# The self neighbour's part of a window graph convolution: per pair from gathered values, or per chunk from y with one matrix

## The reference

```python
feat = concat([x_i, x_j - x_i])          # x_i the node, x_j each of its 9 neighbours
h = einsum('bnkc,oc->bnko', feat, ew) + eb
h = gelu(h * es + et)                    # O = 192 channels
h = max(h, axis=2)                       # over the 9 neighbours
x = affine(conv1x1(window_reverse(h), fc2)) + x
```

## Time and profile before

| | |
|---|---|
| median of 3 runs | 4308.5 us (4302.23 to 4312.94) |
| profiled execution | 4302.27 us, its span 4300.5 us |
| TensorE clock, mean granted | 0.992 |
| busy: PE / DVE / ACT / POOL | 4078.2 / 4077.2 / 3620.3 / 538.3 us (95 / 95 / 84 / 13%) |
| L586 and L592 (self matmuls) | 284.6 and 144.9 us in records of 261 and 219 ns |
| L769 (self GELU) | 262.3 us |
| L941 (maxima) | 992.9 us, 1939 ns each |

### The profile page before, as it was taken

How to read it: one execution, slowest core, us unless ns; L and a number is a source line. 1 busy time by engine, 2 the same in 40 slices (tenths; PEclk the granted TensorE clock), 3 DMA queues, 4 the chain that set the end, 5 groups by cost and what they waited for, 6 DMA issues and landing times.

```text
span 4300.5 us, 84159 instructions
## 1 busy us (share of the span) xinstructions
PE 4078.2 (95%) x26688; PEld 2423.2 (56%) x26688; DVE 4077.2 (95%) x5296; ACT 3620.3 (84%) x7141; POOL 538.3 (13%) x548
## 2 busy tenths in 40 slices
PE   5999999999999999999999999999999999999994
PEld 2555555555555555555555555555555555555552
DVE  2599999999999999999999999999999999999998
ACT  3888888888888888888888888888889888888873
POOL 0011111011111011111011111111111111110100
PEclk9999999999999999999999999999999999999997
DMA  1111121111111111120111111111111111211111
GB/s 48 23 31 33 25 45 18 33 38 30 35 31 31 27 38 32 26 44 16 36 36 24 43 27 32 29 33 34 29 40 20 37 33 25 45 18 25 31 21 24
DMA packets 52989, 134.11 MB, mean 31 GB/s; under 512 B 7778, under 2 KB 9058, under 8 KB 46372
## 3 DMA queue, kind: packets, MB, share of 16 engines
q0 software_dynamic: 28672, 50.35, 8.2%
q1 hardware_dynamic: 23876, 78.22, 6.8%
HBM read 77.68 MB, written 25.69 MB: 24 GB/s over the span
## 4 chain that ended last, share of the span: by engine, by line
PE 61%; ACT 13%; issue 12%; DVE 12%; DMA 0%; SPq 0%; DVEq 0%; ACTq 0%; POOL 0%; POOLq 0%
PE pg L572 15%; DVE acc L954 9%; PE pmisc L498 8%; PE pmisc L482 8%; PE pg L575 7%; PE pvu L559 7%; ACT MV L746 3%; PE pself L586 3%; ACT acc L779 2%; PE pmisc L450 2%; ACT g L763 2%; PE pmisc L500 2%; PE pvu L545 2%; PE pmisc L443 2%; PE pmisc L465 1%
## 5 line engine op out<-in xcount | busy, mean ns | idle before, releaser
L954 DVE SCALAR_TENSOR_TENSOR acc<-hpad,w,acc 128x1024 f32<-128x1024 f32 (+1 forms) x2560 | 2911.9, 1168 | 89.1 <-ACT acc L779 86.0
L572 PE MATMUL pg<-MV,VU 128*128 128x512 f32 x2048 | 1143.8, 640 | 15.6 <-ACT VU L754 14.8
L763 ACT ACTIVATE g<-pg 128x512 f32<-128x512 f32 x1536 | 916.0, 596 | 144.3 <-PE pg L575 75.7
L941 DVE TENSOR_REDUCE hid<-g 128x192 f32<-128x1728 f32 x512 | 992.9, 1939 | 0.0
L746 ACT ACTIVATE MV<-pvu,cst 64x512 f32<-64x512 f32 x1024 | 695.6, 679 | 12.4 <-PE pvu L545 0.2
L482 PE MATMUL pmisc<-x,w 96*128 96x384 f32 (+1 forms) x1536 | 571.6, 487 | 23.1 <-ACT hpad L693 18.5
L575 PE MATMUL pg<-MV,VU 128*64 128x512 f32 x2048 | 527.5, 592 | 0.0
L498 PE MATMUL pmisc<-acc,w 128*96 128x256 f32 x2048 | 494.8, 385 | 30.2 <-ACT acc L786 30.2
L693 ACT ACTIVATE hpad<-pmisc,sh,sc 128x384 f32<-128x384 f32 (+1 forms) x768 | 480.6, 661 | 20.1 <-DVE acc L954 12.7
L559 PE MATMUL pvu<-wVU,y 97*64 97x192 f32 x4096 | 446.6, 339 | 30.6 <-ACT MV L746 30.1
L498 PEld LDWEIGHTS pmisc<-acc,w 128*96 128x96 f32 x2048 | 331.2, 164 | 212.4 <-issue 108.6
(11 more groups left out here) (95 smaller groups left out, 4231.9 us busy)
## 6 DMA issues: line engine op xcount, KB each, us to landing
xin<-in_x_dram SPq DMA_DIRECT2D x32, 768.0 KB, 5.7
invb<-rows_dram SPq DMA_DIRECT2D x32, 768.0 KB
x<-in_x_dram POOLq DMA_DIRECT2D x128, 192.0 KB, 3.6
res<-x POOLq DMA_DIRECT2D x128, 192.0 KB, 3.5
out_dram<-res SPq DMA_DIRECT2D x128, 192.0 KB, 2.1
g<-in_consts_dram SPq DMA_DIRECT2D x1, 640.0 KB
w<-in_p_dram SPq DMA_DIRECT2D x1, 618.5 KB
rows_dram<-norm_rows SPq DMA_DIRECT2D x32, 16.0 KB, 1.4
```

The lines of the kernel that those rows point to most:

```text
L572: last = nc.tensor.matmul(ps[:, :], VU[:, r, part, 0:ONE128], cols[part], start=True, stop=True)
L763: nc.scalar.activation(g[:, p % 2, part, :, 0:KN], pg[(3 * p + part) % 2][:, :].rearrange("p (n k) -> p n k", k=KN), ACT.Gelu).then_inc(ge ...
L941: nc.vector.tensor_reduce(hid[:, c % 2, j, :, :], g[:, r], op=ALU.max, axis=AX.X).then_inc(hid_ready, 1)
L954: nc.vector.scalar_tensor_tensor(out=dst, in0=src, scalar=wk, in1=dst, op0=ALU.mult, op1=ALU.add).then_inc(tap_done, 1)
```

## The change

The self neighbour's part of a node needs no gather: with x_j - x_i zero it is one matrix times y. A third matrix is added to wVU (es times the first half of ew, with the bias row), and two new kinds of shared job, one pair of jobs per chunk (4 pairs of windows): `self_full` multiplies the first 128 channels by all 512 nodes of the chunk, `self_half` the remaining 64 channels by the 256 nodes of each window side, into the two halves of the output partitions. ScalarE applies GELU while it empties the bank, into a new tile gself. They lie in slots 2 and 3 (even chunks) and 4 and 5 (odd chunks) modulo 8, ahead of fc2, w1 and w2 in ORDER.

MV and g lose their ninth place, `self_full`, `self_half` and `gelu_self` of each pair go, and `maxima` reduces over 8 and waits for the last gather's GELU. A new VectorE operation, `join_self`, takes the maximum of the four pairs' hid and gself (two tiles of 128 x 768) once per chunk, right behind the maxima of the chunk's last pair; fc2 waits for it. The transpose gets a bank of its own and loses the wait for the self GELU.

```diff
+SELF_AT = {2: 'self_half', 3: 'self_full', 4: 'self_half', 5: 'self_full'}
+ORDER = ('ssq', 'fc1', 'inv', 'self_full', 'self_half', 'fc2', 'w1', 'w2')
...
+    if p % SLOTS in SELF_AT and valid(b, B):
+        jobs.append((SELF_AT[p % SLOTS], b, p // PPC))
...
-        MV = sb("MV", [128, 2, 2, (KN + 1) * NODES])
-        g = sb("g", [128, 2, 3, NODES, KN + 1])
+        MV = sb("MV", [128, 2, 2, KN * NODES])
+        g = sb("g", [128, 2, 3, NODES, KN])
+        gself = sb("gself", [128, 2, PPC, 3, NODES])
...
+                elif kind == "self_full":
+                    bi, c = job[1:]
+                    last = nc.tensor.matmul(ps[:, :], wVU[:, 2, 0:ONE128], y[:, c, :], start=True, stop=True)
+                elif kind == "self_half":
+                    bi, c = job[1:]
+                    yc = y[:, c, :].rearrange("p (q win n) -> p q win n", q=PPC, win=2)
+                    for w in range(2):
+                        last = nc.tensor.matmul(ps[64 * w:64 * w + 64, 0:PPC * NODES].rearrange("p (q n) -> p q n", q=PPC),
+                                                wVU[:, 2, ONE128:O], yc[:, :, w, :], start=True, stop=True)
...
-                if due(count := P - 2):
-                    pe.wait_ge(self_gelu, count)
...
-            def self_full(P, p):
-                r = p % 2
-                if due(count := P):
-                    pe.wait_ge(self_gelu, count)
-
-                pe.wait_ge(featT_evac, P + 3 if not isinstance(P, int) else min(P + 3, NPAIRS))
-                for w in range(2):
-                    nc.tensor.matmul(pself[:, 64 * w:64 * w + 64], VU[:, r, w, 0:ONE128], MV[:, r, w, KN * NODES:],
-                                     start=True, stop=True)
-
-            def self_half(P, p):
-                r = p % 2
-                for w in range(2):
-                    last = nc.tensor.matmul(pself[64 * w:64 * w + 64, 128:192], VU[:, r, w, ONE128:O],
-                                            MV[:, r, w, KN * NODES:], start=True, stop=True)
-                last.then_inc(self_ready, 1)
...
+                elif kind == "self_full" or kind == "self_half":
+                    bi, c = job[1:]
+                    if kind == "self_half":
+                        if due(count := CHUNKS * bi + c - 1):
+                            act.wait_ge(chunk_ready, count)
...
+                    nc.scalar.activation(dst, src, ACT.Gelu).then_inc(misc_evac, 1)
...
-            def gelu_self(P, p):
-                act.wait_ge(self_ready, P + 1)
-                nc.scalar.activation(g[:, p % 2, :, :, KN],
-                                     pself[:, 0:192].rearrange("p (c n) -> p c n", c=3),
-                                     ACT.Gelu).then_inc(self_gelu, 1)
...
             def maxima(P, p):
                 c, j, r = (p % PAIRS) // PPC, p % PPC, p % 2
-                if due(count := P + 1):
-                    dve.wait_ge(self_gelu, count)
+                if due(count := 3 * P + 3):
+                    dve.wait_ge(gelu_done, count)
                 nc.vector.tensor_reduce(hid[:, c % 2, j, :, :], g[:, r], op=ALU.max, axis=AX.X).then_inc(hid_ready, 1)
+
+            def join_self(b, p, bc, c):
+
+                if due(count := PAIRS * bc + PPC * (c + 1)):
+                    dve.wait_ge(hid_ready, count)
+                fb, fp = when(b, p, 3 if c % 2 else 1)
+                dve.wait_ge(misc_evac, job_at(fb, fp, "self_full", c))
+                dve.sem_inc(dve_passed, 1)
+                nc.vector.tensor_tensor(hid[:, c % 2], hid[:, c % 2], gself[:, c % 2], ALU.max).then_inc(chunk_ready, 1)
...
+                    if p % PPC == 0:
+                        bc, c = (b, p // PPC - 1) if p else (b - 1, CHUNKS - 1)
+                        if valid(bc, B):
+                            join_self(b, p, bc, c)
```

More of the change, by code:

```diff
@@ L48 @@
 TAP_COUNTS = [5, 4, 5, 5, 5, 5, 6, 5]
-ORDER = ('ssq', 'fc1', 'inv', 'fc2', 'w1', 'w2')
+SELF_AT = {2: 'self_half', 3: 'self_full', 4: 'self_half', 5: 'self_full'}
+ORDER = ('ssq', 'fc1', 'inv', 'self_full', 'self_half', 'fc2', 'w1', 'w2')
 ADD_AT = {o + 1: q for o, q in W2_AT.items() if q % 2 == 1}
@@ L194, in build @@
         c16 = sb("c16", [128, C16], f16)
-        wVU = sb("wVU", [C + 1, 2, O])
+        wVU = sb("wVU", [C + 1, 3, O])
         l0sc = sb("l0sc", [C, 2])
@@ L255, in build @@
         pscore = pb("pscore", [128, 512])
-        pself = pb("pself", [128, 512])
+        pfeat = pb("pfeat", [128, 512])
         pvu = pb("pvu", [128, 512])
@@ L276, in build @@
             "featT_ready", "featT_evac", "onehot_in", "onehot_ready"))
-        vu_ready, vu_evac, gather_ready, self_ready, gelu_done, self_gelu = (sem(n) for n in (
-            "vu_ready", "vu_evac", "gather_ready", "self_ready", "gelu_done", "self_gelu"))
+        vu_ready, vu_evac, gather_ready, gelu_done, chunk_ready = (sem(n) for n in (
+            "vu_ready", "vu_evac", "gather_ready", "gelu_done", "chunk_ready"))
         sp_passed, pool_passed, dve_passed = sem("sp_passed"), sem("pool_passed"), sem("dve_passed")
@@ L459, in shared_job @@
                     bc, c = job[1:]
-                    if due(count := PAIRS * bc + PPC * (c + 1)):
-                        pe.wait_ge(hid_ready, count)
+                    if due(count := CHUNKS * bc + c + 1):
+                        pe.wait_ge(chunk_ready, count)
                     hc = hid[:, c % 2]
@@ L529, in feature_transpose @@
                     pe.wait_ge(feat_ready, count)
-                if due(count := P - 2):
-                    pe.wait_ge(self_gelu, count)
                 if due(count := P):
                     pe.wait_ge(featT_evac, count)
-                nc.tensor.matmul(pself[:, 256:320], feat[:, p % 2, :], I2,
+                nc.tensor.matmul(pfeat[:, 0:NODES], feat[:, p % 2, :], I2,
                                  start=True, stop=True).then_inc(featT_ready, 1)
@@ L569, in gather @@
                 r = p % 2
-                cols = [MV[:, r, w, 0:KN * NODES] for w in range(2)]
+                cols = [MV[:, r, w, :] for w in range(2)]
                 if part < 2:
@@ L624, in image @@
                         shared_job(b, p, k, jobs[k])
-                    if valid(P, NPAIRS):
-                        self_full(P, p)
                     if valid(P + 1, NPAIRS):
@@ L630, in image @@
                         gather(P, p, 2)
-                    if valid(P, NPAIRS):
-                        self_half(P, p)
             image_loop(pe, image, TAIL)
@@ L671, in shared_evac @@
                     nc.scalar.activation(norm_rows[:, :], ps[0:8 * PPC, 0:128], ACT.Copy).then_inc(misc_evac, 1)
+                elif kind == "self_full" or kind == "self_half":
[3 more added lines that the diff above has]
+                            act.wait_ge(chunk_ready, count)
+                    if kind == "self_full":
+                        src = ps[:, :].rearrange("p (q win n) -> p q win n", q=PPC, win=2)
+                        dst = gself[:, c % 2, :, 0:2, :]
+                    else:
+                        src = ps[:, 0:PPC * NODES].rearrange("p (q n) -> p q n", q=PPC)
+                        dst = gself[:, c % 2, :, 2, :]
+                    nc.scalar.activation(dst, src, ACT.Gelu).then_inc(misc_evac, 1)
                 elif kind == "fc2":
@@ L731, in featT_copy @@
                     act.wait_ge(onehot_in, count)
-                nc.scalar.activation(featT[:, p % 2, :], pself[:, 256:320], ACT.Copy).then_inc(featT_evac, 1)
+                nc.scalar.activation(featT[:, p % 2, :], pfeat[:, 0:NODES], ACT.Copy).then_inc(featT_evac, 1)
             def feature_square(P, p):
@@ L740, in onehot @@
                 act.wait_ge(onehot_in, P + 1)
-                if due(count := P - 1):
-                    act.wait_ge(self_ready, count)
+                if due(count := 3 * P - 3):
+                    act.wait_ge(gather_ready, count)
                 for w in range(2):
                     h = 64 * w
-                    last = nc.scalar.activation(MV[h:h + 64, p % 2, w, 0:KN * NODES].rearrange("p (n k) -> p n k", k=KN),
+                    last = nc.scalar.activation(MV[h:h + 64, p % 2, w, :].rearrange("p (n k) -> p n k", k=KN),
                                                 pone[h:h + 64, :, :].rearrange("p k n -> p n k"), ACT.Relu,
@@ L762, in gelu @@
                         act.wait_ge(hid_ready, count)
-                nc.scalar.activation(g[:, p % 2, part, :, 0:KN],
+                nc.scalar.activation(g[:, p % 2, part, :, :],
                                      pg[(3 * p + part) % 2][:, :].rearrange("p (n k) -> p n k", k=KN),
                                      ACT.Gelu).then_inc(gelu_done, 1)
-            def gelu_self(P, p):
-                act.wait_ge(self_ready, P + 1)
-                nc.scalar.activation(g[:, p % 2, :, :, KN],
-                                     pself[:, 0:192].rearrange("p (c n) -> p c n", c=3),
-                                     ACT.Gelu).then_inc(self_gelu, 1)
             def tap0(b, p, o, t, gr):
```

(5 more changed lines are left out.)

## The result

The changed kernel takes 4280.7 us (median of 4 runs, 4280.54 to 4282.92) against 4305.4 beside it: a ratio of 0.9941 with a 95% interval of 0.9928 to 0.9953, 20 to 31 us less, where 52 us less were forecast. The direction and the mechanism were right, the size half of what I had worked out. The profiled execution's span is 4281.2 us against 4300.5.

The account below looks back on a forecast made before the run. TensorE and VectorE were taken to bound each half image in turn, VectorE alone after the change. 7.1 us a loop gave 51 us, with start, setup and end 52 us less than 4302.3; 4257 us against the median, range 4233 to 4297.

Parts of the forecast that it names:

- The two regimes before the change: Per half image: VectorE leads from slot 10 to 14 (37.9 us), TensorE in the other eleven slots (92 us).
- The slack: VectorE's wait for tap 0 at slot 10 of each half image, read as 2.35 us in the mean.
- the VectorE sum by halves: VectorE's added work per half: +0.7 us in TensorE's eleven slots, +0.17 in its own five, leaving 1.5 us to gain.
- TensorE's part: Per loop over two images, self matmuls removed (32.0 us) against new shared jobs (21.9 us): 10.1 us less.
- The step that was mis-sized: VectorE's join, once per chunk: 0.98 us each; less 0.81 us of reductions, net +0.17 us a chunk.
- My upper bound, 1.28 us: The dearest join allowed for on VectorE, from a tap of 1024 elements; it would leave 16 us of gain.
- The loop's edge: VectorE's waiting at the edge of the two-image loop, counted as 0.6 us per loop.
- the forecast's own 7.15 loops: The steady part, 3710 us divided by 518.9 us a loop, turning 7.1 us a loop into 51 us.
- Rival 1: TensorE stays the bound because the two half matmuls don't run side by side (1.07 us, not 0.43): 4273 us; chance 0.12.
- Rival 3: ScalarE's self jobs ahead of w1 in slots 2 to 4 delay tap 0, 4.8 us a loop: 4291 us; chance 0.14.
- Rival 2: VectorE already sets the period, so the change only adds 0.17 us a chunk: slower, 4330 us; chance 0.09.
- The rule of the shared port: VectorE and GpSimd lock each other out: one join in four might wait 1.42 us, 45 us in all; not counted.

Follow-up runs that it names:

- Run 5: The kernel before the change, with its maxima over eight of the nine places and nothing else changed: 4282.6 us, ratio 0.9942.
- run 3: The changed kernel with the self jobs and their evacuations cut to 64 columns; join, order and waits stay: 4276.7 us, ratio 0.9920.
- Run 8: The changed kernel with one wait ahead of the join in place of two waits and a semaphore increment: 4257.3 us, ratio 0.9886.
- run 10: The changed kernel without the join: self jobs one chunk earlier, GpSimd copies self values into a ninth place, maxima over nine: 4284.8 us, ratio 0.9949.

## Why the prediction was right in kind and half in size

- The two regimes before the change, and with them the rule that the period shrinks until VectorE no longer waits: right. Run 5 meets the time that follows from them within 2 us. The slack was read a little wrong: of the 34 waits in 79.9 us 28 stand at slot 10, 2.5 us in the mean, and six are others, 1.15 to 2.84 us, each some 20 us behind an edge of the hardware loop. And the VectorE sum by halves counts fifteen reductions for sixteen slots. Neither touches the forecast, which goes by the whole loop.
- TensorE's part: removal and arrival together were forecast at 10.1 us less a loop, 506.1 to 496; it is 495.3. The full job takes 0.94 us in the trace (1030.93 to 1031.87), as taken; the half job 0.58 (1412.76 to 1413.34), not 0.43, between my two ends. With 0.58 the same sum gives 498.5 us, so that the total came out at 495.3 is partly luck: the removal must have been worth more than 32.0 us, and what more isn't shown. Nothing hangs on it (run 3).
- ScalarE: forecast 15.8 us less, measured 6.7. The full evacuation was right (0.596 us), the half one shorter than chosen (0.387 for 0.467), but I had subtracted records of 0.512 us in full, while each overlapped the next: before the change one starts at 1028.89 us and the instruction behind it at 1029.18, 0.29 us later. ScalarE wasn't the bound, so this cost nothing either. I did allow for overlap on VectorE and should have on ScalarE.
- VectorE, the reduction: 0.193 us less a pair, forecast 0.20.
- **The step that was mis-sized is the join's.** Forecast 0.98 us, with 0.12 us for the lost overlap; measured 1.21. The duration was right (0.96 for 0.94). What stands ahead of it was not: I took the dependence from a setup instruction with one wait, and the join has two waits and an increment. Net +0.44 us a chunk, 7 us a loop, where I had 2.7. My upper bound, 1.28 us, did cover it, with 16 us of gain worked out for it.
- The loop's edge costs more after the change than before, 1.5 against 0.6 us on VectorE in the loops shown, which I had left as it was. Most of what is left of the wait for tap 0 belongs to it too: 7.5 of the 8.9 us stand in the six waits some 20 us behind an edge, where TensorE's clock was 0.58 to 0.79 for 8 us, against 0.79 once and 1.00 five times before the change.
- From forecast to result: 4.0 us a loop (511.8 to 515.8), 3.7 of them from the joins. By the forecast's own 7.15 loops that is 29 us, 26 of them from the joins; the gain fell short by 27 (52 to 25). Run 8 shows it from the other side: with the join at 1.01 us the kernel takes 4257.3 us. That this is the forecast to the microsecond is luck in part; its loop is 512.5 us, not 511.8.
- Rival 1 (TensorE still the bound) is ruled out by run 3. Rival 3 (ScalarE's order) is ruled out at its size by the waits: it wanted 4.8 us a loop more of waiting for tap 0, and all such waits are 1.3 us in the loop shown. Run 3 made ScalarE's new work shorter but left its order, so it doesn't test this rival by itself. Rival 2 named the right lever, the price of the join; it was 1.21 us, short of the 1.5 at which the gain would be gone.
- The rule of the shared port, by which one join in four might lose 1.4 us, wasn't put to the test: all 128 joins take 0.957 to 0.960 us, but none of them ran beside a normalise's copy on GpSimd; the nearest was 1.87 us away.

## What to carry to other kernels

When two engines have the same load, price the instruction that the change adds on the second one from start to start: its own duration, the overlap with its neighbours that a dependence takes away, and every wait or increment standing in its engine's queue between it and the instruction it depends on. Put such an instruction one independent instruction later, or give it a single wait: the first gave 16 to 20 us here, the second 24. And an operation added to take work from a reduction must be cheaper than the places it removes: four reductions saved 0.77 us, the join cost 1.21.

## What the runs showed of the hardware that I had not expected

- A second wait and an increment behind an unmet wait delayed the dependent instruction by 0.2 us (0.24 us with two waits and an increment, 0.04 with one wait), about 0.1 us each if they share it evenly, though the semaphore had been met long before. In the written-out steps, where the kernel's wait values are constants and don't hang on the loop's variable, the gap was 0.18 us.
- VectorE lost 0.09 us for each of GpSimd's copies beside it, in run 10. The copies of 192 elements took 0.52 us at the shortest, 1.42 at the median and 1.22 in the mean. The Trainium skill (SBUF — State Buffer, SBUF: two separate sides) has whichever of the two starts first keep the shared port for its whole instruction, while the other is blocked. VectorE's loss is far less than a copy's record, but the longer records may hold time in which the copy was the blocked side, so these runs neither confirm the rule nor refute it.
- The gap of TensorE at the loop's edge, to the first score product, differs by version: before and after, one of six each:

```profile
1337.37 0.34 PE L522 MATMUL pscore<-xn,xs 97*64 97x64 f32 x4 [2.48 <-issue]
```

```profile
1329.81 0.48 PE L535 MATMUL pscore<-xn,xs 97*64 97x64 f32 x4 [3.58 <-issue]
```

It was 2.0 to 2.6 us before, 3.5 to 4.1 after, and 1.6 to 2.3 us in run 10. What sets it was not tried. TensorE's granted clock goes to the lower of its two levels (1.2 GHz of 2.4) behind all six of these gaps in the changed kernel and behind one before it: behind 1329.81 us it was 0.50 for 6 us and a gather's two matmuls took 2.08 us, while behind 1337.37, before the change, it stayed at 1.00 and they took 1.12. The gap's length alone doesn't tell it: the one edge before the change with a lower clock had the shortest gap, 2.04 us.
